# A token reversal moved from the convolution into the attention's steps, and two Toeplitz chunks fetched into memory that the attention has finished with

## The reference, cut to what matters

```python
scores = einsum('bthd,bghd->bhtg', x @ Wq, ctx @ Wk) / sqrt(32)      # 4 heads
topv, topi = top_k(scores, 32); attn = zeros.at[..., topi].set(softmax(topv))
c_t = attn.mean(heads) @ (ctx @ Wv)
x = layernorm(x); scale, shift = split(c_t @ W_film_in + b_film_in)
x = x * (1 + gate * scale) + gate * shift
y = s4d(x, ...)          # causal convolution over the 128 tokens, one kernel per channel
```

## Time and profile before

| | us |
|---|---|
| three runs | 1533.57, 1534.65, 1536.14 |
| median | 1534.65 |
| the profiled execution, its own time | 1533.17 |
| its span | 1531.4 |
| `film_in`, about | 205 to 492 |
| `convolve`, about | 492 to 517 |

### The profile page before, as it was taken

How to read it: one execution, slowest core, us unless ns; L and a number is a source line. 1 busy time by engine, 2 the same in 40 slices (tenths; PEclk the granted TensorE clock), 3 DMA queues, 4 the chain that set the end, 5 groups by cost and what they waited for, 6 DMA issues and landing times. The chain is left out here.

```text
span 1531.4 us, 30812 instructions
## 1 busy us (share of the span) xinstructions
PE 1201.2 (78%) x10533; PEld 812.5 (53%) x10533; DVE 1008.2 (66%) x3914; ACT 684.6 (45%) x1990; POOL 594.7 (39%) x806
## 2 busy tenths in 40 slices
PE   4677654767667678884899897389999969999997
PEld 3433322434434445552677676146666647777765
DVE  7677659999993478853577776557776544444432
ACT  3343334665664434321344453146666643333332
POOL 4677486887875255421222321224334310000000
PEclk8789865566666799986799999579999989898988
DMA  6301050000101401000000000000000000000001
GB/s 164 87 1 42 1 133 1 22 25 15 32 15 58 136 29 42 15 15 14 2 3 3 3 3 3 0 0 2 1 2 1 2 1 1 1 0 0 0 0 55
DMA packets 63678, 35.54 MB, mean 23 GB/s; under 512 B 23925, under 2 KB 61424, under 8 KB 63538
## 3 DMA queue, kind: packets, MB, share of 16 engines
q1 hardware_dynamic: 62234, 33.45, 8.1%
q10 hardware_dynamic: 1304, 0.33, 0.1%
HBM read 25.21 MB, written 6.42 MB: 21 GB/s over the span
## 5 line engine op out<-in xcount | busy, mean ns | idle before, releaser
L2804 DVE SCALAR_TENSOR_TENSOR k_X<-ps,m_gt,k_X 128x128 f32 (+1 forms) x256 | 72.2, 344 | 123.0 <-PE ps L2703 123.0
L2733 ACT ACTIVATE m_hid<-ps,k_b 128x512 f32<-128x512 f32 x128 | 81.8, 684 | 134.9 <-PE ps L2703 127.7
L2703 PEld LDWEIGHTS ps<-k_w,m_hid 128*128 128x128 f32 x1024 | 123.2, 192 | 26.8 <-issue 17.2
L2694 PE MATMUL ps<-m_xnT,k_w 128*128 128x512 f32 x256 | 127.9, 630 | 1.1 <-DVE m_lg L2749 1.1
L2703 PE MATMUL ps<-k_w,m_hid 128*128 128x128 f32 x1024 | 123.4, 275 | 0.0
L2408 POOL TENSOR_TENSOR l_p<-l_p,l_rsum 128x512 f32<-128x512 f32 x64 | 65.2, 1039 | 144.0 <-DVE l_rsum L2641 144.0
L2209 DVE TENSOR_REDUCE g_top<-ps 128x8 f32<-128x1024 f32 x64 | 75.4, 1220 | 50.7 <-PE ps L2077 50.7
L2520 ACT ACTIVATE l_p<-ps,l_shift 128x128 f32<-128x128 f32 x256 | 91.4, 390 | 21.0 <-DVE l_shift L2586 19.8
L1474 DVE MATCH_REPLACE8 c_left<-c_top,c_left 128x128 f32<-128x128 f32 x384 | 100.7, 271 | 0.0
L2157 ACT ACTIVATE g_pT<-ps 128x1024 f32<-128x1024 f32 x64 | 62.1, 1022 | 84.9 <-PE ps L2093 84.9
L711 PE MATMUL ps<-f_expT,f_xeT 128*128 128x512 f32 x128 | 69.9, 675 | 29.3 <-DVE k_X L1089 29.0
(11 more groups left out here) (523 smaller groups left out, 3256.7 us busy)
## 6 DMA issues: line engine op xcount, KB each, us to landing
v_toep<-kpad SPq DMA_DIRECT2D x4, 1024.0 KB, 10.2
fo_dram<-c_fo SPq DMA_DIRECT2D x32, 128.0 KB, 1.7
v_late<-kpad SPq DMA_DIRECT2D x4, 1024.0 KB, 10.4
d_fo<-fo_dram SPq DMA_DIRECT2D x8, 512.0 KB, 3.6
k_X<-in_x SPq DMA_DIRECT2D x8, 256.0 KB, 3.5
out<-k_X SPq DMA_DIRECT2D x4, 512.0 KB, 5.4
f_cx<-in_ctx SPq DMA_DIRECT2D x4, 384.0 KB, 5.1
c_cx<-in_ctx SPq DMA_DIRECT2D x4, 384.0 KB, 4.6
```

What stands on the lines that cost most here:

```text
L2694: pe.matmul(ps[:, 4 * u + q, :], k.w1_3[:, e, 128 * q:128 * q + 128], xnT[:, u], start=True, stop=True).then_inc(s["hid_ps"].sem, 1)
L2703: m = pe.matmul(ps[:, 4 * u + 2 + e % 2, j * S:j * S + S], hid[:, u, q, j * S:j * S + S], k.w2_3[:, e, q, :], start=q == 0, stop=q == 1)
L2733: act.activation(hid[:, u, q, :], ps[:, 4 * u + q, :], ACT.Gelu, bias=k.b1_3[:, 2 * e + q:2 * e + q + 1]).then_inc(s["hid"].sem, 1)
L2804: dve.scalar_tensor_tensor(out=xj[u][j], in0=ps[:, 4 * u + 2 + e % 2, j * S:j * S + S], scalar=gt[:, u, j, e:e + 1], in1=xj[u][j], op0=ALU ...
```

## The change

The flips of `convolve` go. In `film_in`, GpSimd writes the modulated input of an image into a buffer `y` (two images), and after the film products of step p TensorE multiplies `y` of pair p-3 by `k.flip` (256 columns, in bank 7, which the product for `kT` uses too); ScalarE copies the result into `k.x3` behind the film copies. GpSimd waits for the flip of the pair before it writes `y` again. `sc` and `left` get memory that outlives `film_in`, and SP fetches Toeplitz chunk 4 into `sc` between the stores of images 28 and 29, and chunk 5 into `left` between those of images 30 and 31. `convolve` fetches only chunks 6 and 7.

```diff
--- before.py
+++ after.py
@@ -1184,6 +1184,9 @@
         k.toep = ctx.enter_context(nc.sbuf_tensor("v_toep", [128, EARLY, CH, 128], F32))
         once = ctx.enter_context(OneTime(nc, "v_in_"))
         k.toep_in = [once(f"toep_in{i}") for i in range(CHUNKS)]
+
+        k.sc = ctx.enter_context(nc.sbuf_tensor("v_sc", [128, CH, 128], F32))
+        k.left = ctx.enter_context(nc.sbuf_tensor("v_left", [128, CH, 128], F32))
         film_in(nc, w, ps, k)
         convolve(nc, w, ps, k)
 
@@ -1198,6 +1201,7 @@
     PAIRS, GROUPS = B // 2, B // G
     FIRST, LAST = -5, PAIRS + 3
     TAKES = 2 * H * ROUNDS
+    FLIP = 3
     with ExitStack() as ctx:
         def tmp(name, shape, dt=F32):
             return ctx.enter_context(nc.sbuf_tensor("c_" + name, shape, dt))
@@ -1209,7 +1213,8 @@
         qT, kT = tmp("qT", [128, 2, W]), tmp("kT", [128, 2, W])
         onesb = tmp("onesb", [128, 128], BF16)
         minus, tshare = tmp("minus", [128, H]), tmp("tshare", [128, B])
-        sc, left = tmp("sc", [128, 4, H, 128]), tmp("left", [128, 4, H, 128])
+        sc, left = (t[:].rearrange("p (i h) s -> p i h s", h=H) for t in (k.sc, k.left))
+        y = tmp("y", [128, 2, 128])
         exa, exb = tmp("exa", [128, 4, H, 128]), tmp("exb", [128, 2, H, 128])
         first, top = tmp("first", [128, 2, H, 8]), tmp("top", [128, 2, H, 8])
         shift, tota, totb = tmp("shift", [128, 4, H]), tmp("tota", [128, 4, H]), tmp("totb", [128, 2, H])
@@ -1231,6 +1236,7 @@
         wT_ps, wT_done, aT_ps, aT_done, film_ps, fo_done, filmed, x3_done = (
             once(n) for n in ("wT_ps", "wT_done", "aT_ps", "aT_done", "film_ps", "fo_done", "filmed", "x3_done"))
         fo_out = [once(f"fo_out{i}") for i in range(2)]
+        flip_ps, flipped = once("flip_ps"), once("flipped")
         norm = dict(stats=Signal(stats, 0, 2 * G, k.apart), halves=Signal(halves, 0, 6, k.apart),
                     square=Signal(square, 0, 4, k.apart), mean=Signal(mean, 0, 2, k.apart),
                     ve=Signal(ve, 0, 2, k.apart))
@@ -1251,9 +1257,17 @@
                     e = i // 8 + 1
                     sp.wait_ge(aT_ps, 8 * (e - 1))
                     sp.dma_start(cx[:, e % 2], c_dram[:, 8 * e:8 * e + 8, :]).then_inc(cx_in[e], 16)
+                if i == B - 3:
+
+                    sp.wait_ge(left_done, TAKES * (PAIRS - 1) + 2 * H)
+                    sp.wait_ge(exa_done, H * B)
+                    load_toeplitz(sp, k, EARLY, k.sc[:])
                 sp.wait_ge(fo_done, i + 1)
                 sp.dma_start(k.fo_dram[:, i:i + 1, :].rearrange("s b c -> s (b c)"),
                              fo[:, i % 2, 256:512]).then_inc(fo_out[i % 2], 16)
+                if i == B - 2:
+                    sp.wait_ge(exb_done, H * B)
+                    load_toeplitz(sp, k, EARLY + 1, k.left[:])
             for a in range(2):
                 sp.wait_ge(fo_out[a], 16 * B // 2)
 
@@ -1325,8 +1339,9 @@
                     pool.wait_ge(x2c, i // G + 1)
                     pool.tensor_tensor(x2, x2, f[:, 0:128], ALU.mult).then_inc(filmed, 1)
                     pool.wait_ge(filmed, i + 1)
-                    pool.tensor_tensor(k.x3[:, :, i:i + 1], x2.rearrange("p (c o) -> p c o", o=1),
-                                       f[:, 128:256].rearrange("p (c o) -> p c o", o=1), ALU.add).then_inc(x3_done, 1)
+                    if i >= 2:
+                        pool.wait_ge(flip_ps, i // 2)
+                    pool.tensor_tensor(y[:, i % 2, :], x2, f[:, 128:256], ALU.add).then_inc(x3_done, 1)
 
         @block.tensor
         def _(pe):
@@ -1366,6 +1381,8 @@
                     g = (p + 2) // 2
                     if g:
                         pe.wait_ge(kT_done, g)
+                    if p > FLIP:
+                        pe.wait_ge(flipped, p - FLIP)
                     pe.matmul(ps[:, 7, :], k.wk1[:], k.cT[:, W * g:W * g + W], start=True, stop=True).then_inc(k_ps, 1)
                     pe.wait_ge(xT_done, g + 1)
                     pe.matmul(ps[:, 6, :], k.wq1[:], xnT[:], start=True, stop=True).then_inc(q_ps, 1)
@@ -1378,6 +1395,15 @@
                     a = i % 2
                     pe.wait_ge(aT_done, i + 1)
                     pe.matmul(ps[:, 4 + a, :], aT[:, a, :], k.wfilm[:], start=True, stop=True).then_inc(film_ps, 1)
+                if pair(p - FLIP):
+
+                    i = 2 * (p - FLIP)
+                    pe.wait_ge(x3_done, i + 2)
+                    pe.wait_ge(kT_done, min((p + 2) // 2 + 1, GROUPS))
+                    if i:
+                        pe.wait_ge(flipped, i // 2)
+                    pe.matmul(ps[:, 7, 0:256], k.flip[:], y[:].rearrange("p a c -> p (a c)"), start=True,
+                              stop=True).then_inc(flip_ps, 1)
 
         @block.scalar
         def _(act):
@@ -1431,6 +1457,11 @@
                         act.wait_ge(x3_done, i - 1)
                         act.wait_ge(fo_out[i % 2], 16 * (i // 2))
                     act.activation(fo[:, i % 2, :], ps[:, 4 + i % 2, :], ACT.Identity).then_inc(fo_done, 1)
+                if pair(p - FLIP):
+                    i = 2 * (p - FLIP)
+                    act.wait_ge(flip_ps, i // 2 + 1)
+                    act.activation(k.x3[:, :, i:i + 2], ps[:, 7, 0:256].rearrange("p (a c) -> p c a", a=2),
+                                   ACT.Identity).then_inc(flipped, 1)
 
         @block.vector
         def _(dve):
@@ -1480,10 +1511,10 @@
 
 
     with ExitStack() as ctx:
-        late = ctx.enter_context(nc.sbuf_tensor("v_late", [128, CHUNKS - EARLY, CH, 128], F32))
+        late = ctx.enter_context(nc.sbuf_tensor("v_late", [128, CHUNKS - EARLY - 2, CH, 128], F32))
         once = ctx.enter_context(OneTime(nc, "v_"))
         yT = ctx.enter_context(nc.sbuf_tensor("v_yT", [128, 2, CH // 4, 128], F32))
-        flip_ps, flipped, yT_ps, yT_out, y_ps = (once(n) for n in ("flip_ps", "flipped", "yT_ps", "yT_out", "y_ps"))
+        yT_ps, yT_out, y_ps = (once(n) for n in ("yT_ps", "yT_out", "y_ps"))
         block = ctx.enter_context(nc.Block())
 
         def chunk(c):
@@ -1491,18 +1522,16 @@
 
         @block.sync
         def _(sp):
-            for c in range(EARLY, CHUNKS):
-                load_toeplitz(sp, k, c, late[:, c - EARLY])
+            for c in range(EARLY + 2, CHUNKS):
+                load_toeplitz(sp, k, c, late[:, c - EARLY - 2])
 
         @block.tensor
         def _(pe):
-            for c in range(CHUNKS):
-                pe.matmul(ps[:, c, :], k.flip[:], chunk(c), start=True, stop=True).then_inc(flip_ps, 1)
             for n in range(CHUNKS + 1):
                 if n < CHUNKS:
-                    pe.wait_ge(flipped, n + 1)
                     pe.wait_ge(k.toep_in[n], 16)
-                    toep = k.toep[:, n] if n < EARLY else late[:, n - EARLY]
+                    toep = (k.toep[:, n] if n < EARLY else k.sc[:] if n == EARLY else k.left[:] if n == EARLY + 1
+                            else late[:, n - EARLY - 2])
                     for i in range(CH):
                         q, r = i // 4, i % 4
                         m = pe.matmul(ps[B * r:B * r + B, n, 128 * q:128 * q + 128], k.x3[:, CH * n + i, :],
@@ -1517,9 +1546,6 @@
 
         @block.scalar
         def _(act):
-            for c in range(CHUNKS):
-                act.wait_ge(flip_ps, c + 1)
-                act.activation(chunk(c), ps[:, c, :], ACT.Identity).then_inc(flipped, 1)
             for c in range(CHUNKS):
                 act.wait_ge(yT_ps, c + 1)
                 if c >= 2:
```

## The result

The changed kernel takes 1541.37 us (median of 8 runs, 1538.97 to 1544.94), the kernel before, beside it, 1534.9 (8 runs): the medians lie 6.5 us apart. The ratio on record is 1.0032, 95% interval 1.0019 to 1.0045; it is not the quotient of these medians (1.0042), and by it the change costs 4.9 us (2.9 to 6.9). The prediction was 1539.8, slower. The profiled execution took 1541.14, with a span of 1539.2 against 1531.4.

The account below looks back on a forecast made before the run. ScalarE's in-order list, with the TensorE products it waits for, was taken as the bound. Steps +7.0, flips -9.5, store +5.0, clock +2.6 gave +5.1 us: 1539.8 us, slower (chance 0.62); range 1532.5 to 1543, the forecast's own 1537.8 to 1543.

Parts of the forecast that it names:

- ScalarE's list, not VectorE, sets the steps: Attention steps: added product and copy delay the next exponentials, 11 steps x 0.64 = +7.0 us; bounds 3.1 to 9.4.
- GpSimd's wait for the previous flip: Attention steps: before GpSimd rewrites `y`, a new wait some 0.5 us after it would write; priced at nothing.
- Rival A: Attention steps: VectorE at 97% is the real bound and hides the added work; -1.9 us, 1532.7, no change; chance 0.13.
- C: Attention steps cost only 0.28 each, as longer product runs raise the clock or copies overlap; +1.2, 1535.9; chance 0.10.
- The flips' -9.5: Start of `convolve`: with 8 flips and copies gone, Toeplitz products start where flips started, -9.53 us if nothing else moves.
- The store behind chunk 5: End of `film_in`: the last small store queues behind chunk 5, so `convolve` starts at 497.5 instead of 492.50, +5.0 us.
- Rivals B: Steps hide the work and the last store overtakes chunk 5: sum -5.6 us, 1529.0, faster; chance 0.09.
- D: Steps cost 7.0 us but the last store overtakes chunk 5: +1.4 us, 1536.0, no change; chance 0.06.
- the ring rule: SP's queue: each DMA engine consumes descriptors in ring order, so the store starts behind the chunk; without it +1.3, not +5.0.
- The half clock at the first Toeplitz products: Start of `convolve`: TensorE, idle from about 491.5 to 497.5, begins at 1.2 GHz; +2.6 us, bounds 0 and 3.

Follow-up runs that it names:

- experiments 4: Changed kernel with TensorE making every flip's product twice, same values: 1539.98 us, ratio 1.0029 to the kernel before; steps 248.85 us.
- 11: Changed kernel with ScalarE copying every flip's result a second time, into a spare tile: 1545.06 us, ratio 1.0063 to the kernel before; steps 249.27 us.
- Experiment 1: Changed kernel without SP's early fetches, `sc` and `left` back in their old place: 1541.88 us, ratio 1.0056 to the kernel before.
- experiments 2: Kernel before with only `sc` and `left` moved and chunks 4 and 5 fetched early: 1539.68 us, ratio 1.0018 to the kernel before.
- experiment 5: Changed kernel with chunk 5 fetched behind the store of image 31 instead of ahead of it: 1533.18 us, ratio 0.9986 to the kernel before.
- number 6: Changed kernel plus three unread 512-column products on TensorE behind the last flip: 1543.58 us, ratio 1.0047 to the kernel before.
- experiments 3: Changed kernel with flip's product ahead of the `aT` products and its copy ahead of the film copies: 1533.14 us, ratio 0.9990 to the kernel before.

## Why the prediction came out right

The sum was +5.1 us, measured +6.5 by the medians and +4.9 by the ratio; 1541.37 lies in the forecast's own range. The mechanisms of its terms are the ones that the traces show. That the sum fits so well is in part luck: one term was 2.0 too large, and a stage that it left out added 2.2 to 2.7. By terms:

- **ScalarE's list, not VectorE, sets the steps: right.** +7.27 and +7.97 against +7.0. The price of a half-clock step, 0.85 + 0.28 - 0.49, is what the rows show (456.01, 456.86, 457.15), and experiments 4 and 11 show both parts by themselves. Count and price were a little off, and cancel: no step up to the last exponentials had the film wait of 0.26 any more, so 12 (13 in the second trace) and not 11 paid the price of the half clock, 0.61 in the mean. That GpSimd's wait for the previous flip costs nothing is right, though it is up to 1.5 us long and not 0.5. Rival A falls with VectorE's 6.4 us of waits and the longer steps; C with 1.14.
- **The flips' -9.5: right only together with the fetches.** Experiment 1 gets 1.8.
- **The store behind chunk 5: mechanism right, term too large**, +3.0 and +2.9 against +5.0. Chunk 5 was issued 13.2 us after the last exponentials, not 489.1 - 474.5 = 14.6: 1.4, as the last film copy but one follows them after 12.2 us, where it took 13.6 before. It landed after 6.2 us, not after 6.9, the figure of the first of four issued together: 0.7. And the flip's own tail, without the store's, costs nothing either: with the store first the section ends 17.19 after the last exponentials, 0.8 less than before the change. SP's last wait is 4.1 and not about 6, since the issue itself took 1.96 of the 6.0. Rivals B and D fall with it and with experiments 2 and 5. For the ring rule of the Trainium skill (DMA: Bandwidth & Descriptors, "Queues, rings and completion order"), the trace agrees: 6.0 us instead of 1.7 behind a chunk, and 1.0 of wait as soon as the order is turned.
- **The half clock at the first Toeplitz products: right**, 0.50 granted, 9.53 - 7.19 = 2.3 against 2.6. That it goes with the idle time is shown by experiment 5 (1.48 idle, 1.95 us) beside the changed kernel (5.22 idle, 3.64 us), and by number 6 between them (2.57 idle, 3.05 us). That a section which begins with an idle TensorE begins at 1.2 GHz, as the prediction put it, is too general: 1.48 and 2.57 us of idle time left the clock up at the start.
- **Missing: the next stage, +2.2 to +2.7**, which the store's shorter term hid in the sum (5.1 - 2.0 + 0.3 - 0.3 + 2.7 = 5.8, the four stretches together). The prediction put this stage at nothing without naming it. Its place is shown: 1.3 to 1.8 of it is the first load of the film halves; 0.9 comes later in the stage. Its cause is not settled. Queue 8's block goes with it in 8 of 9 traces and is absent in all 5 without the delay, but nothing here moved that block alone.

The one thing that the prediction had wrong in kind is its view of the clock as given: it priced the flip's product in each step at the clock that was there. Rival C's condition, that longer runs of products raise the clock, hardly shows in the changed kernel (0.67, and no film wait of 0.26), where the flip stands at the end of the run, but the clock is higher in experiments 3 and 4 (0.71 and 0.75).

## What to carry to other kernels

Where two engines run abreast, the busy share doesn't say which one leads; ask who waits for whom, and price what is added by its place in the leader's in-order list: behind the film copies the product and copy made the steps 7 us longer, in a gap of the same list the steps came out 5 us shorter than without them, at a higher clock. Before a prefetch is put into a queue, look at what stands behind it: a 128 KB store that closes a section paid for a 1,024 KB chunk, and the idle time it made was paid once more in TensorE's clock. And removing work at a section's start also removes what covered the transfers behind it.

## What the runs showed of the hardware that was not expected

- A path with added TensorE work can come out shorter. With one more product of 256 columns a step ahead of the film products, the granted clock rose from 0.64 to 0.71 and the steps fell from 239.2 to 234.3 us; with the product doubled at the end of the step, the clock was 0.75, and 0.85 us more in each half-clock step came to 1.7 to 2.4 us in all.
- The same products of two chunks took 1.95 us behind 1.48 us without work on TensorE (full clock), 3.05 behind 2.57 (full clock, then the half one from 0.7 us on), and 3.64 behind 4.19 us and more (half clock).
- A store of 128 KB issued right behind a chunk of 1,024 KB on one queue took 1.96 us to issue instead of 0.32 (1.55 to 2.26 in the other traces with that order), and some 6.0 us to land instead of 1.7.
- The first load of a stage was used 4.64 to 5.56 us after its issue in 8 traces in which a block of instructions was fetched beside it on queue 8, and after 3.56 to 3.71 in the 5 without. A ninth trace with such a block did not show it (3.87), and whether the block is the cause is open.
- The recorded mean of one VectorE operation moved between 271 and 394 ns from trace to trace of an unchanged kernel, with no change in the pace of the steps.
